# A two-part kernel on one core: in the stencil, rows across the halves' border by small DMAs, and four products moved to GpSimd

## The reference, cut to what matters

```
Af = A_grid[None] * f[:, None]          # A_grid: 2 grids of 256 x 256
Bf = B_grid[None] * f[:, None]          # B_grid: 3 grids of 256 x 256
gradv_Af  = _grad(Af[:, 0], 1) + _grad(Af[:, 1], 2)
gradvv_Bf = _grad2(Bf[:, 0], 1) + _grad2(Bf[:, 1], 2) + _grad(_grad(Bf[:, 2], 2), 1) + _grad(_grad(Bf[:, 2], 1), 2)
f_new = f + (-gradv_Af + gradvv_Bf * 0.5) * dt[:, None, None]
x = jnp.maximum(f_new, 0.0)
```

## Time and profile before

| what | value |
|---|---|
| median of 3 runs | 368.86 us |
| span of the profiled execution, first to last instruction | 368.1 us |
| stencil in that span, from the first load of Y to the end | about 313 to 368 us |
| busy over the span: PE / DVE / ACT / POOL | 312.2 / 286.2 / 252.8 / 160.1 us |

### The profile page before, as it was taken

How to read it: one execution, slowest core, us unless ns; L and a number is a source line. 1 busy time by engine, 2 the same in 40 slices (tenths; PEclk the granted TensorE clock), 3 DMA queues, 4 the chain that set the end, 5 groups by cost and what they waited for, 6 DMA issues and landing times.

```text
span 368.1 us, 7195 instructions
## 1 busy us (share of the span) xinstructions
PE 312.2 (85%) x2304; PEld 283.9 (77%) x2304; DVE 286.2 (78%) x517; ACT 252.8 (69%) x463; POOL 160.1 (44%) x114
## 2 busy tenths in 40 slices
PE   1757314789999999999999999999999996099996
PEld 1646314689999999999999999999999996034342
DVE  4988791688878878877886887887788692599993
ACT  2659014398899789789889978978988861197112
POOL 1445303152555654553554565455355414066540
PEclk9999855699999999999999999999999999579999
DMA  7902433894777875875877777576574400786513
GB/s 276 362 2 88 142 126 127 282 347 146 276 271 251 286 244 171 280 245 187 275 263 267 257 277 247 173 265 233 189 275 148 151 4 29 244 249 129 121 57 115
DMA packets 49780, 74.31 MB, mean 202 GB/s; under 512 B 3293, under 2 KB 40543, under 8 KB 49632
## 3 DMA queue, kind: packets, MB, share of 16 engines
q1 hardware_dynamic: 45056, 62.13, 49.6%
q0 software_dynamic: 4368, 11.54, 10.5%
q10 hardware_dynamic: 336, 0.39, 0.3%
HBM read 63.56 MB, written 9.31 MB: 198 GB/s over the span
## 4 chain that ended last, share of the span: by engine, by line
PE 72%; DVE 15%; DMA 6%; issue 2%; POOL 2%; ACT 1%; SPq 0%; DVEq 0%; POOLq 0%
PE psum L964 31%; PE psum L942 24%; PE psum L990 6%; PE psum L935 5%; PE psum L911 2%; DMA x_sb<-in_x_dram 2%; PE psum L937 2%; DMA raw_b<-in_L_cond_exp_w_dram 2%; PE psum L898 1%; DVE st L1072 1%; DMA t_y<-y_rows 1%; DVE z L1062 1%; POOL rs L722 1%; DVE t_b0f L1406 1%; PE psum L858 1%
## 5 line engine op out<-in xcount | busy, mean ns | idle before, releaser
L739 POOL DMA_INDIRECT gathered<-h_rows,src_cur x40 | 78.6, 1965 | 123.5 <-DVE src_cur L1238 66.1
L964 PE MATMUL psum<-w_split,hid 128*128 128x256 f32 x936 | 117.8, 285 | 0.2 <-issue 0.2
L964 PEld LDWEIGHTS psum<-w_split,hid 128*128 128x128 f32 x936 | 113.7, 192 | 0.3 <-issue 0.3
L942 PE MATMUL psum<-slot_h,w_split 128*128 128x256 f32 x768 | 96.5, 286 | 3.0 <-DVE slot_h L1255 3.0
L942 PEld LDWEIGHTS psum<-slot_h,w_split 128*128 128x128 f32 x768 | 94.7, 194 | 3.5 <-issue 3.5
L1249 DVE TENSOR_TENSOR w_split<-raw_b,w_split 128x2048 fp32r<-128x2048 f32 x23 | 52.7, 2293 | 22.3 <-ACT w_split L566 21.3
L589 ACT ACTIVATE relu<-psum,b_cur 128x256 f32<-128x256 f32 x128 | 53.6, 488 | 13.2 <-PE psum L942 10.9
L1243 DVE TENSOR_TENSOR w_split<-raw_a,w_split 128x2048 fp32r<-128x2048 f32 x23 | 52.5, 2282 | 8.1 <-DMA gathered<-h_rows,src_cur 7.0
L598 ACT ACTIVATE hid<-relu 128x512 fp32r<-128x512 f32 (+1 forms) x92 | 50.9, 588 | 9.6 <-DVE relu L1261 9.6
L752 POOL DMA_INDIRECT y_rows<-y_sb,dst_cur x39 | 43.1, 1106 | 27.1 <-issue 11.4
L1272 DVE TENSOR_TENSOR hid<-relu,hid 128x512 fp32r<-128x512 f32 x64 | 42.0, 687 | 10.0 <-ACT hid L598 9.4
(11 more groups left out here) (167 smaller groups left out, 357.4 us busy)
## 6 DMA issues: line engine op xcount, KB each, us to landing
raw_a<-in_L_cond_exp_w_dram SPq DMA_DIRECT2D x23, 1024.0 KB
raw_b<-in_L_cond_exp_w_dram SPq DMA_DIRECT2D x23, 1024.0 KB
t_y<-y_rows SPq DMA_DIRECT2D x6, 512.0 KB, 8.4
x_sb<-in_x_dram SPq DMA_DIRECT2D x4, 512.0 KB, 7.8
h_rows<-h_tok SPq DMA_DIRECT2D x16, 128.0 KB, 2.2
x_sb<-t_y POOLq DMA_DIRECT2D x4, 512.0 KB, 4.7
out_dram<-t_out SPq DMA_DIRECT2D x3, 512.0 KB, 2.9
b_all<-in_L_cond_exp_b_dram SPq DMA_DIRECT2D x1, 1024.0 KB, 10.5
```

The costliest lines, as they stand in the source:

```text
L739: pool.indirect_dma_start(out=gathered[:, par, t, :], out_offset=None, in_=h_rows, in_offset=bass.IndirectOffsetOnAxis(ap=src_cur[:, par, ...
L942: last = pe.matmul(banks[bank][:, ST * (blk % 2):ST * (blk % 2) + rows], w_split[:, 0, par, w, at:at + P], slot_h[:, par, h, k, 0:rows], s ...
L964: last = pe.matmul(banks[bank][:, D * t:D * t + D], hid[:, par, h, blk, P * t:P * t + P], w_split[:, 1, par, w, D * blk:D * blk + D], star ...
```

## The change

The products that only carried a row across the halves' border go. `along_rows` keeps the product of a half with itself (2 instead of 4). In exchange SyncE copies, for each pair, the one border row of each half of U2 and U1 into a small tile NEXT (4 DMAs of one partition and 2 KB; rows 0 to 3 of the tile hold them, the rest is zero), and TensorE multiplies NEXT once per half with a matrix that has the two border coefficients (`next_rows`, 2 products). The table of constants grows by 256 columns. GpSimd takes GF of pair 0 from VectorE, and the own products A0 dt f of pairs 1 to 3; for these ScalarE makes A0 dt (AD) ahead of time, and keep(1) moves ahead of FD(0). TensorE does columns(0) behind D2(1) and next_rows(0), and GF(0) and GF(3) right before their SM. center(g) no longer waits for U1.

The diff, cut to its core:

```
--- before.py
+++ after.py
+C_NEXT = C_EDGE + 24
+C_ALL = C_NEXT + KD * P
...
+            AD = {g: own(f"t_a0dt_{g}", [P, 4 * D])[:, :] for g in range(1, NB // 2)}
+            NEXT = [own(f"t_next_{par}", [P, 2 * D]) for par in range(2)]
... SyncE
+            def rows_next(g):
+                par = g % 2
+                if g >= 2:
+                    sp.wait_ge(t_mm, g - 1)
+                else:
+                    sp.wait_ge(next_clear, par + 1)
+                for n, (u, ready) in enumerate(((U2, t_u2), (U1, t_u1))):
+                    sp.wait_ge(ready, g + 1)
+                    for q, row in ((0, 0), (1, P - 1)):
+                        sp.dma_start(NEXT[par][2 * q + n:2 * q + n + 1, :]...,
+                                     u[par][row:row + 1, :]...[:, :, 1 - q, :]).then_inc(next_in[par], 16)
+            rows_next(0)
             for g in range(NPAIR - 1):
+                rows_next(g + 1)
                 sp.wait_ge(t_relu, g + 1)
                 sp.dma_start(out_tok[:, 4 * g:4 * g + 4, :], ...)
... ScalarE
             keep(0)
+            keep(1)
+            for g in range(1, NPAIR):
+                for i in range(2):
+                    last = act.activation(AD[g][:, 512 * i:512 * i + 512],
+                                          grid[:, 0, :, :].rearrange("p q d -> p (q d)"), ACT.Copy,
+                                          scale=dt_b[:, 2 * g + i:2 * g + i + 1])
+                last.then_inc(t_ad, 1)
... GpSimd
+            def own_columns(g):
+                whole(g)
+                pool.wait_ge(t_ad, g)
+                if g >= 2:
+                    pool.wait_ge(t_u1, g - 1)
+                pool.tensor_tensor(PA[g % 2], AD[g], field(g), ALU.mult).then_inc(t_a, 1)
+            for par in range(2):
+                pool.memset(NEXT[par][:, :], 0.0).then_inc(next_clear, 1)
+            center(0)
             plus(1, 0)
             plus(1, 1)
             add_y1(2)
-            center(1)
+            own_columns(1)
             add_y2(2)
             add_y1(3)
+            center(1)
+            own_columns(2)
+            add_y2(3)
             center(2)
-            add_y2(3)
             merge(1)
+            own_columns(3)
             pool.wait_ge(t_s_pool, 1)
             center(3)
             merge(2)
... TensorE
                 for q in range(2):
-                    for k in range(2):
-                        at = col + T * k + P * q
-                        rows_mm(g, q, cst[:, at:at + P], u[g % 2], k, start=start and k == 0)
+                    at = col + T * q + P * q
+                    rows_mm(g, q, cst[:, at:at + P], u[g % 2], q, start=start)
+            def next_rows(g):
+                pe.wait_ge(next_in[g % 2], 64 * (g // 2 + 1))
+                for q in range(2):
+                    pe.matmul(banks[2 * (g % 2) + q], cst[:, C_NEXT + P * q:C_NEXT + P * q + P], NEXT[g % 2][:, :], ...)
             def columns(g):
                 if MERGED[0] <= g < MERGED[1]:
                     pe.wait_ge(t_s_pool, g)
                 else:
+                    pe.wait_ge(t_gf_pool, g + 1)
+                    for q in range(2):
+                        rows_mm(g, q, ident, GF[g % 2], q)
                     pe.wait_ge(t_s, g + 1)
...
-                if g in (0, NPAIR - 1):
-                    pe.wait_ge(*((t_gf, 1) if g == 0 else (t_gf_pool, g)))
-                    for q in range(2):
-                        rows_mm(g, q, ident, GF[g % 2], q, start=True)
                 pe.wait_ge(t_u2, g + 1)
-                along_rows(g, C_D2, U2, start=(MERGED[0] <= g < MERGED[1]))
-                if g >= 2:
+                along_rows(g, C_D2, U2, start=True)
+                if g >= 1:
+                    next_rows(g - 1)
                     columns(g - 1)
                 pe.wait_ge(t_u1, g + 1)
                 along_rows(g, C_D1, U1)
-                if g == 0:
-                    columns(g)
+            next_rows(NPAIR - 1)
             columns(NPAIR - 1)
... VectorE, products(g)
                 if g == 0: ...
                 else:
-                    first_of_rows()
-                    link(own_columns())
+                    link(first_of_rows())
+                    dve.wait_ge(t_a, g)
                     rows_out()
                     link(both_columns())
             for g in range(NPAIR):
-                if g == 0:
-                    center_first()
                 products(g)
```

More of the change, by code:

```diff
@@ L42 @@
 C_EDGE = C_D2 + KD * T
-C_ALL = C_EDGE + 24
+C_NEXT = C_EDGE + 24
+C_ALL = C_NEXT + KD * P
 def width(s):
@@ L82, in constants @@
     d1, d2 = stencil(T)
+    for q in range(KD):
+        row, other = (P - 1, P) if q == 0 else (P, P - 1)
+        for n, m in enumerate((0.5 * d2, d1)):
+            c[2 * q + n, C_NEXT + P * q + row % P] = m[row, other]
     c[:, C_D1:C_D1 + KD * T] = d1.T.reshape(KD, P, T).transpose(1, 0, 2).reshape(P, -1)
@@ L329, in moe_then_stencil @@
         t_f, t_u2 = sem("t_f"), sem("t_u2")
-        t_u1, t_s, t_gf, t_mm, t_relu = (sem(n) for n in ("t_u1", "t_s", "t_gf", "t_mm", "t_relu"))
+        t_u1, t_s, t_mm, t_relu = (sem(n) for n in ("t_u1", "t_s", "t_mm", "t_relu"))
         y1_added = {g: sem(f"y1_added{g}") for g in range(2, NB // 2)}
@@ L335, in moe_then_stencil @@
         t_gf_pool, t_s_pool = sem("t_gf_pool"), sem("t_s_pool")
+        t_ad, t_a = sem("t_ad"), sem("t_a")
+        next_clear = sem("next_clear")
+        next_in = [sem(f"next_in{par}") for par in range(2)]
         out_dma = [sem(f"out_dma{i}") for i in range(3)]
@@ L460, in _ @@
                                  y_rows_tok[c, :, 4 * g:4 * g + 4, :]).then_inc(y_in[c][g], 16)
+            def rows_next(g):
[7 more added lines that the diff above has]
+                    for q, row in ((0, 0), (1, P - 1)):
+                        sp.dma_start(NEXT[par][2 * q + n:2 * q + n + 1, :].rearrange("p (i d) -> p i d", i=2),
+                                     u[par][row:row + 1, :].rearrange("p (i q d) -> p i q d", i=2, q=KD)[:, :, 1 - q, :]
+                                     ).then_inc(next_in[par], 16)
+            rows_next(0)
             for g in range(NPAIR - 1):
+                rows_next(g + 1)
                 sp.wait_ge(t_relu, g + 1)
@@ L652, in keep @@
             def keep(g):
[L654 to L657, removed]
+                if g >= 2:
+                    act.wait_ge(t_gf_pool, g - 1)
                 for i in range(2):
@@ L691, in _ @@
                     gated(1)
-                if g < NPAIR - 1:
+                if 1 <= g < NPAIR - 1:
                     keep(g + 1)
@@ L784, in add_y2, with whole @@
                 pool.dma_start(field(g), Y2[g], accum_op=ALU.add).then_inc(y2_added[g], 16)
-            def center(g):
-                if g == 1:
+            def whole(g):
+                if g == 0:
+                    pool.wait_ge(t_f, 1)
+                elif g == 1:
                     pool.wait_ge(t_f_pool, 2)
@@ L790, in center @@
                     pool.wait_ge(y2_added[g], 16)
+            def center(g):
+                whole(g)
                 pool.wait_ge(t_keep, g + 1)
-                pool.wait_ge(t_u1, g)
-                if g == 2:
-                    pool.wait_ge(t_mm, 1)
+                if g >= 2:
+                    pool.wait_ge(t_mm, g - 1)
                 pool.tensor_tensor(GF[g % 2], GG[g % 2], field(g), ALU.mult).then_inc(t_gf_pool, 1)
+            def own_columns(g):
+                whole(g)
+                pool.wait_ge(t_ad, g)
+                if g >= 2:
+                    pool.wait_ge(t_u1, g - 1)
+                pool.tensor_tensor(PA[g % 2], AD[g], field(g), ALU.mult).then_inc(t_a, 1)
             def merge(g):
                 pool.wait_ge(t_s, g + 1)
-                pool.wait_ge(t_gf_pool, g)
+                pool.wait_ge(t_gf_pool, g + 1)
                 pool.tensor_tensor(SM[g % 2], SM[g % 2], GF[g % 2], ALU.add).then_inc(t_s_pool, 1)
+            for par in range(2):
+                pool.memset(NEXT[par][:, :], 0.0).then_inc(next_clear, 1)
+            center(0)
             plus(1, 0)
@@ L994, in along_rows @@
                 for q in range(2):
-                    for k in range(2):
-                        at = col + T * k + P * q
-                        rows_mm(g, q, cst[:, at:at + P], u[g % 2], k, start=start and k == 0)
+                    at = col + T * q + P * q
[3 more added lines that the diff above has]
+                for q in range(2):
+                    pe.matmul(banks[2 * (g % 2) + q], cst[:, C_NEXT + P * q:C_NEXT + P * q + P], NEXT[g % 2][:, :],
+                              start=False, stop=False)
             def columns(g):
@@ L1393, in rows_of @@
                 return v.rearrange("p (r d) -> p r d", d=D)
[L1395 to L1398, removed]
             def products(g):
@@ L1419, in own_columns @@
                 def own_columns():
+                    assert g == 0
                     return dve.tensor_tensor(wide(a), over(A0), wide(f), ALU.mult)
```

## The result

The changed kernel takes 378.17 us (median of 4 runs, 377.59 to 379.74), the kernel before on the same chip 368.76: a ratio of 1.0252 [1.0227 to 1.0277]. The forecast was 374.0 us, the range 368.4 to 375.9. Slower was right and the lock was where it had been placed; the size was not: +9.4 us instead of +5.1.

What follows compares the result with a forecast made beforehand. VectorE's chain up to U2(3), then TensorE's products behind it, were taken as the bound. Delays of U2 (+2.0, +3.3, +3.9) and 28 instructions behind U2(3) gave +5.1 on 368.86: 374.0 us, range 368.4 to 375.9.

Steps and rivals of the forecast that it cites:

- the lock: Stencil, pairs 0 to 2: GpSimd products and two-SBUF-operand VectorE instructions exclude each other; U2(3) 3.9 us later.
- The start: Ahead of U2(0): moving center_first off VectorE gives 0.4 us; keep and AD on ScalarE cost zero.
- the 0.76 us between span and median: Whole run: the median lies 0.76 us above the span of 368.1, and both move alike.
- TensorE's clock is a cost on top: D1(0) may start at 1.2 GHz, losing up to 2.5 us in pair 0; U2(2) up to 1.4 later, 375.4.
- the saving on TensorE: 44 products become 36, 6.9 us less work, had only where TensorE is what is waited for.
- not blocked: VectorE in the stencil isn't held by GpSimd's products: 368.9, with the clock loss up to 371.5; chance 0.17.
- work taken out pays: FD(3) not held by ReLU(1), VectorE's 3.8 us all come, U2(3) at 348.5: 366.3 us; chance 0.13.
- late copy: At the end next(3) waits for U1(3)'s rows, landing after 4.7 instead of 2.2 us: 376.2; chance 0.05.

Runs made afterwards that it cites:

- e3: The changed kernel with all-zero products put into three of TensorE's pauses (behind D2(0), D1(1), D1(2)); 375.81 us, ratio 1.0183 to the kernel before.
- e2: The changed kernel with four products in along_rows again and no row copies; 376.69 us, ratio 1.0199 to the kernel before.
- e6: The changed kernel with the GpSimd windows of e4 and the two altered orders of e5 together; 372.55 us, ratio 1.0091 to the kernel before.
- e7: e6 plus three all-zero products behind D2(0), and pair 3 with four products and no copies; 370.71 us, ratio 1.0033 to the kernel before.
- e5: The changed kernel with ScalarE doing FD(g) ahead of ReLU(g-2) and TensorE finishing pair g-1 ahead of D2(g); 376.85 us, ratio 1.0205.
- e8: The kernel before with only the row copies and NEXT products added, in its own order; 370.73 us, ratio 1.0044 to the kernel before.
- e9: e7 with pair 0's GF product moved into TensorE's pause behind D2(0), ahead of two all-zero products; 369.78 us, ratio 1.0012 to the kernel before.
- e10: e9 with VectorE also adding GF(2) into SM(2), two products fewer on TensorE; 368.48 us, ratio 0.9978 to the kernel before.
- e11: e9 with VectorE adding GF into SM for pairs 1 and 2; 369.89 us, ratio 1.0021 to the kernel before.
- e4: The changed kernel with GpSimd's own(g) held until behind SM(g-1), center(g) behind U1(g), and no merges; 377.4 us, ratio 1.0202.

## Why the prediction was wrong

- The lock: right in place and price. U2(1) 333.60 (forecast 333.75), blocks of 2.06 and 2.05 at U1(0) and U1(1) (2.08 and 2.05), 0.97 at first(1) (0.65), 1.90 at first(2) (2.05). The figure of the Trainium skill weighed there ("SBUF — State Buffer", section "A bandwidth-pool intuition that's wrong (but worth ruling out)": "blocked until DVE-end + ~115 ns") stands on that page beside a DMA that waits for GpSimd's descriptors behind a VectorE copy. It does not carry over: VectorE is free 0.13 or 0.14 us ahead of the product's end in all five, not behind it.
- The start: 0.4 us were to come from center_first, and keep and AD on ScalarE were to cost nothing. U2(0) came at 321.64, forecast 321.67.
- Two readings in the working were off without touching the sum. Of U2, b, own, pf and qf four and not five lie beside plus(1,0) and plus(1,1), since U2(0) ends at 323.32. And the 0.76 us between span and median are no constant: in the runs below an execution of the kernel before takes 1.6 to 1.7 us more than its own span, so the one that was profiled took about 369.8 us, by this estimate.
- The step that failed is "TensorE's clock is a cost on top": the fall was counted once, ahead of D1(0), with at most 1.4 us, through ReLU and FD(2), and left out of the 374.0. It fell three times. In pair 0 it moved TensorE's end to 343.76 instead of 342.07 (e3), so center(2) started late enough to hold SM(1) for 2.03 instead of 0.3 us: U2(2) 1.84 late. FD(2), the path that had been named, was done at 346.01, ahead of U2(2) at 347.29. In pair 1, D2(2) and next(1) at 1.2 GHz took 6.71 instead of 3.84 us, and through ReLU(1) and FD(3) U2(3) waited 1.28. In the last pair D2(3) and next(2) took 5.57 instead of 3.84. That is 1.84 + 1.28 + 1.73 = 4.85; TensorE ended at 374.54, 4.89 behind the forecast's 369.65.
- Why it was missed: the saving on TensorE was called worthless where TensorE waits. It was worse: 36 products instead of 44, in pairs that the lock had made longer, left pauses of 5.91, 3.17 and 2.00 us, and behind each the clock fell. With 44 products and the locks (e2) it fell once. In the kernel before the clock stays at 1.00 from 328 us to the end of the products, and TensorE's longest pause there is the 0.66 us ahead of D1(0):
```profile
328.00:364.50 36.50, 35.43 (x81) 14.77 (x80) 33.81 (x40) 14.91 (x26) 16.42 (x10) 1.00 0.43 101
```
- By the medians e3 is 6.05 over before, by the spans 5.1. Of the 0.95 between them 0.77 is that the profiled execution of e3 (375.04) is the shortest of its four, and 0.2 lies outside the span, as in every run with copies.
- Rival "not blocked": not the case. Rival "work taken out pays": e6 and e7 are its place, U2(3) before 351.0. It would still not have paid as priced, since TensorE's list then starts to bound. Rival "late copy": not in the changed kernel, whose TensorE never stood before a NEXT product; it shows where TensorE comes to NEXT sooner (0.47 to 1.74 us in e5, e8, e9, e10 and e11).

## What to carry to other kernels

Work taken off an engine that waits for another's output buys pauses, and on TensorE a pause can cost: check each one that the change makes longer, in every repetition, and price the products behind it at 1.2 GHz too. Its length alone does not tell whether the clock falls (e4, two pauses of 2.00 us). Where several limits lie within a few us of each other, undoing one shows little (1.8 to 3.4 us of 9.4 here, and two together 6.4); test them in pairs before calling one harmless. In these runs GpSimd products of this size cost VectorE least when they started where its next 2 us read PSUM (e6, e7: at most 0.2 us each).

## What the runs showed of the hardware

- After the change, each of five VectorE instructions with two SBUF operands that started in a GpSimd product of 128x1024 float32 was held until 0.13 or 0.14 us before that product's end, and then took its usual 1.2 us; one with an operand in PSUM was not held (U2(2), 1.21 us at 347.29, with merge(1) from 347.45 to 349.80).
- Products with an all-zero matrix in its pauses kept TensorE's granted clock at 1.00 from 329 us to the end of the products (e3). The Trainium skill (TensorE: Matmul & The Clock Gate, "What's actually happening") puts the price of the clock's rise at under 1% of a typical span. The medians agree, 3.4 of 378 us or 0.9%, but the rows of the profiled execution do not: the three falls add up to 4.85 of 379.74 us, 1.3%.
- The product that waited for two 2 KB copies of one partition by SyncE started 3.0 us after the first of their issues in e8 (358.60 to 361.59), and 5.1 us after it in e11 (337.76 to 342.84), where the share of the DMA engines was 0.98 meanwhile. No run takes that other traffic away, so what makes the difference is not shown. The two issues alone took 1.15 (e8) and 1.52 us (e11).
